# First transformer layer as one stream of 64 pairs of heads, with the scores formed a second time with keys on partitions, and softmax weights kept in fp32

## The chip, the cores and the metric

One core of a Trainium2 chip runs the whole program in one launch. The metric is the device time in microseconds (us), median of several executions of the same program. TensorE multiplies matrices into PSUM (8 banks of 128 partitions x 512 fp32), VectorE (DVE), ScalarE (ACT) and GpSimd (POOL) do the elementwise work, and SyncE (SP) issues the DMA transfers. PEld in the profile is TensorE's load of the stationary operand, PE its product.

## The reference, cut to what matters

Two transformer layers over `x` of shape (4, 512, 512). The change touches the first one only: attention with 32 heads of width 16 that share one key and one value head, a linear position bias, a causal mask, and then a linear layer.

```python
x = x + _layernorm(_L0_attn_ref(_layernorm(x), Wq, Wkv, Wo))
x = x + _layernorm(_L0_ffn_ref(_layernorm(x), q_scales, q_vals, bias))

# _L0_attn_ref
q = (hidden_states @ Wq).reshape(b, s, 32, 16)
kv = hidden_states @ Wkv
k, v = kv[..., :16], kv[..., 16:]
scores = jnp.einsum('bqhd,bkd->bhqk', q, k) * scale
bias = slopes[:, None, None] * (pos[None, None, :] - pos[None, :, None])
scores = jnp.where(causal[None, None], scores + bias[None], -jnp.inf)
attn = jax.nn.softmax(scores, axis=-1)
out = jnp.einsum('bhqk,bkd->bqhd', attn, v).reshape(b, s, h)
return out @ Wo
```

## The kernel before

The program has four parts in time: a stage that splits the weights into fp16 high and low halves (`split_matrices`, line 181) and multiplies two fp32 matrices of the second layer (`FusedUpProjections.multiply`, line 796); `layer0` (line 193); the attention of the second layer; its feed-forward part. Only `layer0` is touched.

Every product of activations and weights runs in fp16 as three passes, high x high, low x high, high x low (`product`, line 398). Every transpose is a TensorE instruction on fp32 data against an identity, evacuated twice: ScalarE writes the high half, VectorE subtracts it and writes the low half.

`layer0` calls `run(b, attend, back, front)` for b = -1, 0, 1 and 2 (a hardware loop), 3, 4. A call with `attend` computes the heads of batch b, and, dealt out over its steps, the output projection and linear layer of batch b-1 (`back`) and the first normalisation of batch b+1 (`front`). Between calls all engines meet in `clear`. One step handles one head:

- `stack_queries` (lines 443 and 444, once per two heads) copies the queries of two heads into 128 rows; ScalarE evacuates them at line 535.
- `scores` (line 459) multiplies by the stacked keys, queries on partitions, 512 + 384 + 256 + 128 columns, the causal triangle of 128-blocks.
- GpSimd makes the table of position biases and mask (line 371); VectorE adds it to the score, writes the sum to SBUF and takes the row extreme in the same instruction (`biased`, line 680).
- ScalarE takes the exponential in SBUF with the extreme as bias (line 575).
- TensorE transposes the ten 128x128 blocks (line 472); ScalarE (line 543) and VectorE (line 708) write the fp16 high and low halves to `pT`.
- `weigh_values` (line 484) forms 30 products per head, each with a 128x128 fp16 block of weights as stationary operand and 17 columns of values (16 and a column of ones for the row sum) as moving operand; ScalarE copies the 68 columns to `ob` (line 550).

Sums are divided out per batch (lines 649 and 652). Layer normalisations are VectorE's work (statistics, line 592; scaling, line 603; addition, line 612), except that GpSimd computes the power -1/2 (line 359) and scales `x_front` (line 363). PSUM banks go round in the order of a list of uses: a use takes the bank that the use eight places before it has left, and `take(u)` waits until that one is evacuated.

Of the kernel before, what the change touches and what calls it, by code (L numbers as in the profile page):

```python
# [29 lines left out]
ALU = mybir.AluOpType  # L30
# [8 lines left out]
P = 128  # L39
# [153 lines left out]
def layer0(nc, A, W0, C, xT, x2_dram):  # L193
# [5 lines left out]

    with ExitStack() as stack:  # L200
        sc = Scope(nc, stack)
        xb = sc.sb("xb", [P, TT, D])
        yb = sc.sb("yb", [P, TT, D])
        xf = sc.sb("x_front", [P, TT, D])
        aT = [sc.sb("front_T_hi", [P, KT, S], F16), sc.sb("front_T_lo", [P, KT, S], F16)]
        bT = [sc.sb("back_T_hi", [P, KT, S], F16), sc.sb("back_T_lo", [P, KT, S], F16)]
        khi = sc.sb("khi", [P, S], F16)
        kst = sc.sb("kst", [P, S], F16)
        kab = sc.sb("kab", [P, 2, S], F16)
        v2 = sc.sb("v2", [P, TT, 2 * EV], F16)  # L210
        qT = [sc.sb("qT_hi", [P, KT, S], F16), sc.sb("qT_lo", [P, KT, S], F16)]
        stk = sc.sb("stk", [P, 2, S], F16)
        tab = sc.sb("tab", [P, 4, S])
        xp = sc.sb("xp", [P, 4, TRIW])
        pT = [sc.sb("pT_hi", [P, 3, NBLK, P], F16), sc.sb("pT_lo", [P, 3, NBLK, P], F16)]
        ob = sc.sb("ob", [P, TT, H0, EV])
        nm = sc.sb("nm", [P, 4, TT])
        rsum = sc.sb("rsum", [P, TT, H0])
        st = sc.sb("st", [P, TT, 6])
# [3 lines left out]
        cs = sc.sb("cs", [P, 1])  # L223
        cinv = sc.sb("cinv", [P, 1])
        cy = sc.sb("cy", [P, 1])
        banks = [sc.ps(f"bank{i}", [P, S]) for i in range(8)]

        s_x = sc.sem("s_x_loaded")
        s_dv = sc.sem("s_dve_steps")
        s_ya = sc.sem("s_y_out")  # L230
        s_yf = sc.sem("s_y_filled")
        s_xf = sc.sem("s_front_loaded")
        s_nf = sc.sem("s_front_normed")
        s_kv = sc.sem("s_keys_values_ready")
        s_ve = sc.sem("s_variance")
        s_rs = sc.sem("s_rstd")
        s_xn = sc.sem("s_normed_rows")
# [3 lines left out]
        s_sf = sc.sem("s_s_filled")  # L241
        s_sh = sc.sem("s_s_hi_out")
        s_kf = sc.sem("s_stack_filled")
        s_sd = sc.sem("s_s_freed_by_dve")
        s_sa = sc.sem("s_stack_ready")
        s_tab = sc.sem("s_table")
        s_ex = sc.sem("s_exp")
        s_pf = sc.sem("s_pv_filled")
        s_pd = sc.sem("s_pv_out")
        s_on = sc.sem("s_heads_normed")  # L250
        s_out = sc.sem("s_x_stored")

        def score_fills(h):

            return [("s", h, i) for i in range(3 - h % 2)]

        def score_fill(h, t):

            return ("s", h - h % 2, 2) if t == 1 else ("s", h, 0 if t == 3 else 1)

        Q_AT = {0: 1, 9: 2, 11: 3}
        Y_AT, N2_AT = (1, 3, 5, 7), (12, 13, 14, 15)
        F_AT, N3_AT = (17, 19, 21, 23), (28, 29, 30, 31)
        N1_AT = (16, 18, 20, 22)

        wq, wkv, wo, wf = W0["wq"], W0["wkv"], W0["wo"], W0["wf"]
        GQ, GKV, GO, GF = range(4)  # L270
        gm = W0["gm"]

        def run(b, attend, back, front):

            extra = {}
            if attend:
                extra.update({h: [("q", m)] for h, m in Q_AT.items()})
                if back:
                    for kind, at in (("y", Y_AT), ("n2", N2_AT), ("f", F_AT), ("n3", N3_AT)):
                        extra.update({h: [(kind, t)] for t, h in enumerate(at)})  # L280
                if front:
                    extra.update({h: [("n1", t)] for t, h in enumerate(N1_AT)})

                front_pieces = {2: (0,)}
                back_pieces = {8: (0,), 9: (1,), 10: (2,), 24: (3,), 25: (4,), 26: (5,)}
                pool_pieces = {2: ["n1"]} if front else {}
                if back:
                    pool_pieces.update({8: ["rstd"], 9: ["rstd"], 24: ["rstd"], 25: ["rstd"]})
                steps = H0 + 2
            else:  # L290
                for h, kind in enumerate(("y", "n2", "f", "n3") * back + ("n1",) * front):
                    extra[2 * h] = [(kind, t) for t in range(TT)]
                front_pieces = {-1: (0,)}
                back_pieces = {1: (0, 1, 2), 5: (3, 4, 5)}
                pool_pieces = {0: ["rstd"] * (front + 4 * back)}
                steps = 8 if back else 2

            uses = [("K",), ("V",), ("q", 0)] * attend + [("o", t) for t in range(TT)] * back
            uses += ([("stack", 0)] + score_fills(0)) * attend
            for h in range(steps):
                if attend:
                    uses += [("T", h - 1, i) for i in range(3)] * (1 <= h <= H0)
                    uses += [("stack", h // 2 + 1)] * (h % 2 == 0 and h // 2 + 1 < PAIRS)
                    uses += [("pv", h - 2)] * (h >= 2)
                    uses += score_fills(h + 1) if h + 1 < H0 else []
                uses += extra.get(h, [])
            slot = {u: n for n, u in enumerate(uses)}  # L310


            signals = {k: (s_tf, s_tl) for k in ("n1", "T", "o", "n2", "n3")}
# [1632 lines left out]
```

## Time and profile before

| | us |
|---|---|
| median of 3 executions | 2516.77 |
| lowest, highest | 2516.7, 2525.8 |
| the profiled execution, its own time | 2520.12 |
| its span, first to last instruction | 2518.3 |
| granted TensorE clock, mean over the span | 0.944 of full speed |

The span is the part of the profiled execution that the trace divides; 1.8 us lie around it. Rows of a stretch give, in order: its bounds, its length, the busy time of PE, PEld, DVE, ACT and POOL with the number of instructions, the granted TensorE clock (1.00 is 2.4 GHz, 0.50 is 1.2 GHz), the share of the DMA engines and GB/s. A group of instructions gives line, engine, operation, tiles, shapes and count, then busy time, mean duration in ns, and the idle time of the engine before them with its releaser.

### The profile page before, as it was taken

The numbers are of one execution on the slowest core, as the hardware profiler recorded it, in microseconds if no ns is written. First come the engines' busy times: TensorE is split into PE (matmuls) and PEld (weight loads), VectorE is DVE, ScalarE is ACT, GpSimd is POOL, SyncE is SP. The second block draws the span as 40 slices with busy tenths as digits, with TensorE's granted clock in tenths as the row PEclk, the third lists the DMA queues.
The fourth block names the chain that finished last, engine by engine and source line by source line (L and its number), as shares of the span: only waits on it lengthen the run. The fifth ranks groups of instructions, "written<-read, shape, count | busy, mean of one in ns | idle before, by whom it ended". The sixth has DMA issues, their size and how long they took to land. (4 is left out here: it accounts for less than half of the span.)

```text
span 2518.3 us, 49756 instructions
## 1 busy us (share of the span) xinstructions
PE 2146.9 (85%) x18352; PEld 1310.3 (52%) x18352; DVE 1864.5 (74%) x4645; ACT 1531.5 (61%) x3606; POOL 688.4 (27%) x563
## 2 busy tenths in 40 slices
PE   6688777778774589999999999999999999758997
PEld 2465555555552255555555555655555556423443
DVE  3688897897995477777777777777777777575554
ACT  2587776777771376667667676667666767341221
POOL 0312212111110243343433343334333333112221
PEclk9899899889997799999999999999999999978999
DMA  5101001000000343444334434443344333320000
GB/s 203 33 2 35 1 7 47 2 18 18 2 18 17 115 81 63 89 87 91 80 66 89 81 71 82 80 91 78 64 89 84 66 68 65 72 87 17 34 17 34
DMA packets 380593, 147.59 MB, mean 59 GB/s; under 512 B 354928, under 2 KB 359664, under 8 KB 378304
## 3 DMA queue, kind: packets, MB, share of 16 engines
q1 hardware_dynamic: 380352, 144.41, 25.5%
q8 instruction: 147, 2.41, 0.4%
q14 instruction: 94, 0.77, 0.1%
HBM read 48.95 MB, written 11.53 MB: 24 GB/s over the span
## 5 line engine op out<-in xcount | busy, mean ns | idle before, releaser
L1157 ACT ACTIVATE xp<-xp,nm 128x128 f32<-128x128 f32 (+3 forms) x512 | 281.3, 550 | 354.5 <-DVE nm L1236 354.5
L1017 POOL TENSOR_TENSOR q_in_sbuf<-q_in_sbuf,sinq 128x512 f32<-128x512 f32 x128 | 231.2, 1806 | 688.2 <-ACT q_in_sbuf L1145 581.3
L1207 DVE SCALAR_TENSOR_TENSOR probs_lo<-xp,rl,probs_hi 128x128 f16<-128x128 f32 (+3 forms) x512 | 263.5, 576 | 109.4 <-ACT probs_hi L1122 109.4
L575 ACT ACTIVATE xp<-xp,nm 128x512 f32<-128x512 f32 (+3 forms) x512 | 249.8, 569 | 50.9 <-DVE nm L680 49.1
L680 DVE CUSTOM_DVE_ANT_0 xp<-bank,tab,cs 128x512 f32<-128x512 f32 (+3 forms) x512 | 250.2, 545 | 4.3 <-PE bank L459 2.0
L1236 DVE CUSTOM_DVE_ANT_0 xp<-bank,mask,cs 128x128 f32<-128x128 f32 (+3 forms) x512 | 250.3, 545 | 0.0
L1122 ACT ACTIVATE probs_hi<-xp,rl 128x128 f16<-128x128 f32 (+3 forms) x512 | 244.0, 549 | 0.7 <-DVE rl L1256 0.7
L472 PE MATMUL bank<-ident,xp 128*128 128x128 f32 x1280 | 182.7, 291 | 62.6 <-ACT xp L575 45.6
L1041 PE MATMUL bank<-xT_hi,wq_hi 128*128 128x512 f16 x512 | 195.2, 381 | 43.2 <-DVE yacc L1251 37.4
L708 DVE TENSOR_TENSOR pT_lo<-bank,pT_hi 128x384 f16<-128x384 f32 (+1 forms) x384 | 207.1, 593 | 32.5 <-ACT pT_hi L543 32.4
L1041 PE MATMUL bank<-p1T_hi,v_hi 128*128 128x128 f16 x1280 | 223.0, 220 | 2.9 <-DMA p1T_lo<-probs_lo 2.9
L1041 PE MATMUL bank<-p1T_hi,v_lo 128*128 128x128 f16 x1280 | 222.9, 220 | 0.0
L1041 PE MATMUL bank<-p1T_lo,v_hi 128*128 128x128 f16 x1280 | 222.8, 220 | 0.0
L543 ACT ACTIVATE pT_hi<-bank 128x384 f16<-128x384 f32 (+1 forms) x384 | 181.0, 537 | 57.0 <-PE bank L472 55.0
L1024 POOL TENSOR_TENSOR qf<-q_in_sbuf,t 128x512 f32<-128x512 f32 x160 | 204.3, 1277 | 31.2 <-POOL q_in_sbuf L1017 19.0
L472 PEld LDWEIGHTS bank<-ident,xp 128*128 128x128 f32 x1280 | 150.4, 148 | 99.9 <-issue 27.9
L371 POOL TENSOR_SCALAR tab<-rel,cinv 128x512 f32<-128x512 f32 x128 | 92.5, 725 | 390.0 <-DVE nm L680 318.3
L1041 PE MATMUL bank<-xT_hi,wq_lo 128*128 128x512 f16 x512 | 195.2, 381 | 0.0
L1041 PE MATMUL bank<-xT_lo,wq_hi 128*128 128x512 f16 x512 | 195.0, 381 | 0.0
L1041 PE MATMUL bank<-wo_hi,o1T_hi 128*128 128x512 f16 x512 | 194.0, 379 | 1.1 <-issue 1.1
L1041 PE MATMUL bank<-wo_lo,o1T_hi 128*128 128x512 f16 x512 | 194.0, 379 | 0.0
L1041 PE MATMUL bank<-wo_hi,o1T_lo 128*128 128x512 f16 x512 | 194.0, 379 | 0.0
(235 smaller groups left out, 5535.9 us busy)
## 6 DMA issues: line engine op xcount, KB each, us to landing
raw_q<-in_wq SPq DMA_DIRECT2D x8, 1024.0 KB, 5.3
raw_o<-in_wo SPq DMA_DIRECT2D x8, 1024.0 KB, 5.6
x_front<-in_x SPq DMA_DIRECT2D x4, 1024.0 KB, 5.8
xb<-in_x SPq DMA_DIRECT2D x4, 1024.0 KB, 7.1
x_scratch<-xb SPq DMA_DIRECT2D x4, 1024.0 KB, 4.4
x_before<-x_scratch SPq DMA_DIRECT2D x4, 1024.0 KB, 5.6
wup<-in_wup SPq DMA_DIRECT2D x3, 1024.0 KB, 11.9
fused_scratch<-fused SPq DMA_DIRECT2D x12, 256.0 KB, 2.4
```

The costliest lines, as they stand in the source:

```text
L472: last = pe.transpose(bank[:, at:at + P], xp[:, h % 4, TRI[t] + j * P:TRI[t] + (j + 1) * P], C["ident"][:, :])
L543: act.activation(pT[0][:, h % 3, COLD[js[0]]:COLD[js[0]] + n, :], bank_of(("T", h, i))[:, 0:n * P].rearrange("p (t c) -> p t c", c=P), ACT ...
L575: act.activation(x, x, ACT.Exp, scale=-1.0, bias=nm[:, h % 4, t:t + 1]).then_inc(s_ex, 1)
L680: ins = dve.tensor_tensor_reduce(out=xp[:, h % 4, TRI[t]:TRI[t] + w], in0=bank_of(u)[:, at:at + w], in1=tab[:, h % 4, S - w:S], scale=cs[: ...
L708: dve.tensor_tensor(pT[1][:, h % 3, c, :], bank_of(u)[:, 0:n * P].rearrange("p (t c) -> p t c", c=P), pT[0][:, h % 3, c, :], ALU.subtract) ...
L1017: pool.tensor_tensor(qs[:, i % 2, :], qs[:, i % 2, :], rope["sink" if u[0] == "k" else "sinq"][:, :], ALU.mult).then_inc(s_rot, 1)
L1024: pool.tensor_tensor(qf[:, i % 2, :], qs[:, i % 2, :], t2[:, i % 2, :], ALU.add).then_inc(s_qf, 1)
L1041: ins = pe.matmul(out, lhs(a), rhs(c), start=(first and i == 0), stop=(last and i == 2))
L1122: ins = act.activation(pr[0][:, m % 2, c], xp[:, m % 3, c], ACT.Copy, scale=rl[:, m % 3, t:t + 1])
L1157: ins = act.activation(x, x, ACT.Exp, scale=-1.0, bias=nm[:, m % 3, t:t + 1], accum_out=ls[:, m % 3, t:t + 1])
L1207: ins = dve.scalar_tensor_tensor(pr[1][:, m % 2, c], xp[:, m % 3, c], rl[:, m % 3, t:t + 1], pr[0][:, m % 2, c], ALU.mult, ALU.subtract)
L1236: ins = dve.tensor_tensor_reduce(out=xp[:, m % 3, TRI[t]:TRI[t] + w], in0=bank_of(("s", m, i))[:, col:col + w], in1=mask[:, S - w:S], scal ...
```

## The change

`layer0` is rewritten; the rest of the program is untouched. Its calls of `run` become one block without a barrier, a loop over steps n = -16 to 91. Pair p of heads (64 in all, 16 per batch) passes through it in three places: scores and maxima at step p, exponents at step p + 6, products with the values at step p + 7. Each step also holds one piece of the other work of some batch.

- Scores are formed with queries on partitions, only for their maximum. The query stack holds, per head, 64 rows: the high and low halves, the slope beside a row of positions, and rows for the maximum. It is put together by 24 DMAs per four pairs instead of by TensorE and ScalarE. The position bias is thus part of the product. The mask is written to the bank by a product of a diagonal with a triangle before it. The two heads of a pair use rows 0 to 63 and 64 to 127 of the array.
- VectorE takes the maxima with five reductions of 512 columns per pair, and writes nothing else. The maxima of four pairs are transposed once, split in halves and put into the query stack by four DMAs.
- The scores are formed again with keys on partitions, minus the maximum through those rows: the exponents, already transposed. ScalarE takes five exponentials of 512 columns per pair straight from PSUM and writes fp32 weights `px`. Tables, transposes and both halves of `pT` are gone.
- `weigh_values` uses the fp32 weights as they are: 20 products per pair, stationary 128x128 fp32, 17 moving columns of fp32.
- Layer normalisations scale on ScalarE, add on GpSimd; the division by the sums is on GpSimd.

The diff, cut to its core:

```diff
-            uses = [("K",), ("V",), ("q", 0)] * attend + [("o", t) for t in range(TT)] * back
-            uses += ([("stack", 0)] + score_fills(0)) * attend
...
+        X_LAG, V_LAG, N_LAG = 6, 7, 8
+        for n in STEPS:
+            if 0 <= n < NP:
+                fillings += [("s", n, i) for i in range(5)]
+            if 0 <= n - V_LAG < NP:
+                fillings.append(("pv", n - V_LAG))
+            if n % GP == 0 and 0 <= n // GP - 1 < NG:
+                fillings.append(("m", n // GP - 1))
+            if 0 <= n - X_LAG < NP:
+                fillings += [("x", n - X_LAG, i) for i in range(5)]
+            fillings += others(n)
...
+                def take(u):
+                    i = place[u]
+                    if i >= 8:
+                        pe.wait_ge(*emptied[fillings[i - 8]])
+                    return banks[i % 8]
...
+                def weigh_values(p):
+                    out = take(("pv", p))
...
+                    pe.wait_ge(*emptied[("x", p, 4)])
+                    for e in range(2):
+                        for t in range(TT):
+                            for j in range(t + 1):
+                                i, c = block_of(e, j, t)
+                                ins = pe.matmul(out[:, (TT * e + t) * EV:(TT * e + t + 1) * EV], px[:, p % 3, i, c:c + P],
+                                                v2[:, p // PAIRS % 2, j, :], start=(j == 0), stop=(j == t))
...
+                for n in STEPS:
+                    if 0 <= n < NP:
+                        mask_scores(n)
+                        scores(n)
+                    if 0 <= n - V_LAG < NP:
+                        weigh_values(n - V_LAG)
+                    if n % GP == 0 and 0 <= n // GP - 1 < NG:
+                        turn_maxima(n // GP - 1)
+                    if 0 <= n - X_LAG < NP:
+                        mask_exponents(n - X_LAG)
+                        exponents(n - X_LAG)
+                    for u in others(n):
+                        fill(u)
...
+                for n in STEPS:
+                    for u in others(n - 1):
+                        evacuate(u)
+                    for u in norms_at(n):
+                        normalise(u)
+                    if 0 <= n - X_LAG < NP:
+                        exponentials(n - X_LAG)
+                    if 0 <= n - V_LAG < NP:
+                        copy_heads(n - V_LAG)
```

The first loop over steps is TensorE's, the second ScalarE's. `mask_scores` and `mask_exponents` take their five banks, one product each of 128 or 256 columns (1024 in all), before the eight products of `scores` or `exponents` (2560 columns in all). `exponentials` waits for the first two banks together and for the other three together.

## Rows read from the trace of the kernel before

**Rows 1.** The page: the span, and the busy share of each engine.

```profile
span 2518.3 us, 49756 instructions
...
PE 2146.9 (85%) x18352; PEld 1310.3 (52%) x18352; DVE 1864.5 (74%) x4645; ACT 1531.5 (61%) x3606; POOL 688.4 (27%) x563
```

**Rows 2.** Busy time, clock, DMA by stretch: stage start, second batch, tail, first layer.

```profile
62.00:80.00 18.00, 6.15 (x22) 4.15 (x23) 7.71 (x17) 2.39 (x4) 3.50 (x5) 0.50 0.26 66
...
219.00:398.00 179.00, 142.44 (x1692) 99.88 (x1692) 159.42 (x455) 127.39 (x299) 37.46 (x41) 0.91 0.06 19
...
759.00:827.00 68.00, 33.06 (x144) 19.70 (x144) 39.25 (x81) 9.92 (x16) 4.04 (x4) 0.71 0.09 32
62.00:827.00 765.00, 575.57 (x6768) 404.72 (x6768) 639.01 (x1824) 510.47 (x1192) 137.76 (x160) 0.89 0.05 18
```

**Rows 3.** Groups by line and shape, VectorE: line, names, shapes, count, busy us, mean ns, idle.

```profile
L708 DVE TENSOR_TENSOR pT_lo<-bank,pT_hi 128x384 f16<-128x384 f32 x256 | 130.3, 549 | 31.7 <-ACT pT_hi L543 31.6
...
L592 DVE BATCH_NORM_STATS2 st<-yb 128x6 f32<-128x512 f32 x32 | 19.7, 680 | 11.1 <-ACT yb L563 11.0
```

**Rows 4.** The same view, TensorE products and weight loads (PEld).

```profile
L472 PE MATMUL bank<-ident,xp 128*128 128x128 f32 x1280 | 182.7, 291 | 62.6 <-ACT xp L575 45.6 <-DVE qT_lo L644 12.7 <-DVE pT_lo L708 2.4
L472 PEld LDWEIGHTS bank<-ident,xp 128*128 128x128 f32 x1280 | 150.4, 148 | 99.9 <-issue 27.9 <-DVE pT_lo L708 19.6 <-DVE nm L680 16.6
...
L484 PE MATMUL bank<-v,pT_hi 128*128 128x17 f16 x2560 | 116.9, 171 | 21.8 <-DVE nm L680 16.6 <-DVE pT_lo L708 4.8
...
L484 PEld LDWEIGHTS bank<-v,pT_hi 128*128 128x128 f16 x2560 | 112.5, 97 | 31.1 <-DVE nm L680 18.1 <-DVE pT_lo L708 6.3 <-issue 0.8
```

**Rows 5.** Line 796, the fp32 product: durations min, median, max; then two weight loads.

```profile
L796 PEld LDWEIGHTS fu_bank<-wup,wdk x96: 186/190/337, 9.1 to 54.4; 128*128 128x128 f32 x96
L796 PE MATMUL fu_bank<-wup,wdk x96: 592/592/1194, 9.1 to 54.8; 128*128 128x512 f32 x96
...
30.02 0.19 PEld L796 LDWEIGHTS fu_bank<-wup,wdk 128*128 128x128 f32 x1 [0.24 <-issue]
30.45 0.19 PEld L796 LDWEIGHTS fu_bank<-wup,wdk 128*128 128x128 f32 x1 [0.24 <-issue]
```

**Rows 6.** Timeline (start, length, engine, line): ten transposes; two fp16 products.

```profile
113.36 1.15 PEld L472 LDWEIGHTS bank<-ident,xp 128*128 128x128 f32 x10 [0.79 <-issue]
113.39 1.35 PE L472 MATMUL bank<-ident,xp 128*128 128x128 f32 x10 [0.48 <-ACT xp L575]
...
80.88 0.38 PE L398 MATMUL bank<-front_T_hi,wkv_hi 128*128 128x512 f16 x1
...
81.10 0.38 PE L398 MATMUL bank<-front_T_hi,wkv_lo 128*128 128x512 f16 x1
```

**Rows 7.** ScalarE: timeline of eight copies and of four exponentials; then two groups.

```profile
40.71 3.99 ACT L803 ACTIVATE fused<-fu_bank 128x512 f32<-128x512 f32 x8
...
300.14 1.90 ACT L575 ACTIVATE xp<-xp,nm 128x512 f32<-128x512 f32 x4
...
L550 ACT ACTIVATE ob<-bank 128x68 f32<-128x68 f32 x128 | 29.6, 231 | 7.6 <-PE bank L484 7.4
...
L563 ACT ACTIVATE yb<-bank,cy 128x512 f32<-128x512 f32 x16 | 11.0, 688 | 23.4 <-PE bank L398 23.4
```

**Rows 8.** Stretches before and after two falls of the granted clock (seventh column).

```profile
114.50:117.90 3.40, 2.33 (x39) 1.43 (x38) 2.58 (x11) 2.87 (x6) 2.19 (x4) 1.00 0.00 0
118.00:121.00 3.00, 3.00 (x41) 2.53 (x40) 3.00 (x10) 2.37 (x7) 0.69 (x2) 0.50 0.02 5
...
282.00:285.30 3.30, 0.00 (x0) 0.00 (x0) 3.27 (x6) 0.20 (x1) 0.00 (x0) 0.99 0.00 0
286.00:289.00 3.00, 1.83 (x33) 1.10 (x33) 2.97 (x14) 1.70 (x3) 2.02 (x3) 0.50 0.00 0
```

**Rows 9.** The first score evacuation of the layer, VectorE's timeline.

```profile
88.82 0.75 DVE L680 CUSTOM_DVE_ANT_0 xp<-bank,tab,cs 128x512 f32<-128x512 f32 x1 [1.97 <-PE bank L459]
```

More of the change, by code:

```diff
@@ new lines, in layer0 @@
+        far = sc.sb("far", [P, P], F16)
+        tri = sc.sb("tri", [P, 2, P], F16)
+        trit = sc.sb("tri_T", [P, 2, P], F16)
+        row = {n: sc.sb(f"row_{n}", [P, 1]) for n in ("hi", "lo", "pos", "max")}
+        sl = sc.sb("slopes", [P, H0])
+        slh = sc.sb("slopes_hi", [P, H0], F16)
+        slq = sc.sb("slopes_32", [P, 2, H0])
+        col = sc.sb("slope_rows", [P, PAIRS])
+        unit = sc.sb("unit", [P, 1])
+        runit = sc.sb("runit", [P, 1])
+        fq = sc.sb("fq", [P, 1])
@@ L251, in layer0 @@
         s_out = sc.sem("s_x_stored")
[L253 to L270, printed above, removed]
@@ new lines, in _, with hi4, evacuate @@
+            @block.scalar
+            def _(act):
+                act.wait_ge(s_st, 1)
+                act.wait_ge(s_io, 1)
+                for i in range(PAIRS):
+                    ins = act.activation(qs[:, i // GP, i % GP, :], pos[:, :], ACT.Identity, scale=0.0,
+                                         bias=col[:, i:i + 1])
+                ins.then_inc(s_st, 1)
+                def hi4(u):
+                    act.wait_ge(*filled[u])
+                    kind, b, t = u
+                    if t == 0 and kind == "n1" and b >= 2:
+                        act.wait_ge(*filled[("q", GP * (b - 2) + 3)])
+                    if t == 0 and kind == "o" and b >= 1:
+                        act.wait_ge(*last_of("f", b - 1))
+                    if t == 0 and kind == "n2":
+                        act.wait_ge(*last_of("y", b))
+                    act.activation(transposed(u, 0), bank_of(u)[:, :].rearrange("p (k c) -> p k c", c=P),
+                                   ACT.Copy).then_inc(s_th, 1)
+                def evacuate(u):
+                    kind, b = u[0], u[1]
+                    if kind in ("n1", "o", "n2", "n3"):
+                        hi4(u)
+                    elif kind == "K":
@@ new lines, in normalise @@
+                def normalise(u):
+                    kind, b = u
+                    src = {"n1": xf, "a1": yb, "a2": yb, "n2": xb, "n3": xb}[kind]
+                    dst = xf if kind == "n1" else yb
+                    act.wait_ge(s_rs, norm_no[u] + 1)
+                    if kind in ("n2", "n3"):
+                        act.wait_ge(s_ad, TT * (add_no["a" + str(int(kind[1]) - 1), b] + 1))
+                    for t in range(TT):
+                        act.activation(dst[:, t, :], src[:, t, :], ACT.Identity, scale=rs[:, t:t + 1],
+                                       bias=nb[:, t:t + 1]).then_inc(s_nm, 1)
@@ new lines, in exponentials, with copy_heads @@
+                def exponentials(p):
+                    if p >= 3:
+                        act.wait_ge(s_pf, p - 2)
+                    for i in range(5):
+                        act.wait_ge(*filled[("x", p, i)])
+                        act.activation(px[:, p % 3, i, :], bank_of(("x", p, i))[:, :], ACT.Exp,
+                                       scale=unit[:, 0:1]).then_inc(s_ed, 1)
+                def copy_heads(p):
+                    g, pp = p // GP, p % GP
+                    act.wait_ge(*filled[("pv", p)])
+                    if g >= 2 and pp == 0:
+                        act.wait_ge(s_on, g - 1)
+                    act.activation(ob[:, g % 2, 2 * pp:2 * pp + 2, :, :].rearrange("p h t e -> p (h t e)"),
+                                   bank_of(("pv", p))[:, 0:2 * TT * EV], ACT.Copy).then_inc(s_pd, 1)
```

942 lines of the change are left out of this document (510 added, 432 removed).

## The prediction

> **What bounds the kernel now.** I read the page first: 2518.3 us, with PE busy 85% and DVE 74% over the whole program [rows 1]. That is an average over stages with different limits, so the second view is the stretches. The first layer is 62 to 827 us, 765 us long: DVE 639 us busy, PE 576, ACT 510 [rows 2]. In the second batch's 179 us DVE is busy 159 (89%), PE 142, ACT 127 at a granted clock of 0.91 [rows 2]: VectorE ends the steps. The groups say with what. Per head it evacuates ten transposed blocks and the scores; the three-block subtraction alone is 256 x 549 ns [rows 3]. Attention, from 80 to 759 us, is 679 us for 64 pairs of heads: 10.6 us a pair, with everything dealt in between. That is the number to beat.
>
> **What comes off VectorE, ScalarE and GpSimd.** DVE loses both evacuations of a pair and gains five reductions of 512 columns. A 512-column read of fp32 took it 680 ns [rows 3], so 5 x 0.68 = 3.4 us at most. ACT: five exponentials. Eight PSUM copies of 512 columns took 3.99 us together at 0.60 for the last, 0.48 us each back to back; four exponentials over 1280 columns with a pointer operand took 1.90; one copy with a pointer scale 688 ns [rows 7]. I take 0.55 us from start to start and 0.69 for the last: 4 x 0.55 + 0.69 = 2.9 us (2.6 by the copies, 3.4 at 5 x 0.69). The copy of 136 columns is 231 ns for 68 [rows 7] plus some, 0.3. Neither engine alone bounds a step: 3.4 and 3.2 us, plus about 1 to 3 us of other pieces, are under 10.6. GpSimd's table goes. Normalisations now on ACT and POOL, and the DMAs of the stacks, have four steps or a whole step of slack; I cost them at nothing. Their cover is the time in which ACT waits for TensorE (below); without it each 512-column scaling costs 0.69 us.
>
> **What comes onto TensorE.** fp16 products of 512 columns start 0.22 us apart at full clock (80.88, 81.10) [rows 6], so 0.43 ns a column. Per pair: masks 2 x 1024 columns, 2 x 0.44 us. Scores and exponents 2560 columns each: 1.10 us one after the other. If the products on the two halves of the array run side by side, the widest of each pair (512 + 384 + 384 + 256) gives 0.66. No row shows such products; I take 1.0 and keep 0.66 to 1.1. By the Trainium skill (TensorE: Matmul & The Clock Gate, Part 3, Packing small matmuls) products on distinct row groups run concurrently; that would be the lower end, and no run here shows it yet.
>
> The weights are the heavy term. Line 796 is the one fp32 product of the trace: 48 products give 96 records, so each fp32 product is two loads and two products, 40 of each a pair. Its load takes 190 ns at full clock, against 97 for fp16 and 148 for the fp32 transposes [rows 4, 5]. If what the fp16 load takes is fixed time, the fp32 load holds the array for the rest, 190 - 97 = 93 ns, and somewhat more. It hides while a product of 512 columns runs (start to start 430 ns) [rows 5]. With 17 moving columns there is nothing to hide it behind. The ten transposes went 1.15 us for ten loads, 0.11 us apart [rows 6]. I take 0.115 us a load, 40 x 0.115 + 0.2 for the first = 4.8 us a pair. Bounds: 0.06, as (148 - 97) would say if this load ran like a transpose's, 2.5 us; and 0.19, every load unhidden, 7.8 us. What it replaces took 60 fp16 products and 20 transposes a pair. The Trainium skill (same page, Weight-path perf modes) says that the fast weight load doesn't work for fp32; by its load of 128 columns at 1.2 per ns the term would be 4.3 us, an estimate. The rows 190 against 97 agree in direction.
>
> **What of it lies on the path.** Two places tie the engines. TensorE's order in step n is: score masks, scores(n), values(n-7), exponent masks, exponents(n-6), other work. Scalar's: exponentials(n-6), then the copy of the values' bank of n-7. Step n+1's third score mask takes the bank eight places back, which is that values' bank. So scores(n+1) can't start until ACT has done all five exponentials of step n and the copy; and values(n+1) wait for the fifth exponential of step n too. ACT in turn has no exponents until TensorE has gone through scores, values and masks. The two alternate. A period, at full clock:
>
> - exponent masks and the first two banks, with two drains and a semaphore: 0.44 + 0.35 + 0.3 = 1.1 us
> - ACT: 2.9 + 0.3 = 3.2 us
> - three score masks, scores, drain: 0.35 + 1.1 = 1.45 us
> - values: 4.8 us
>
> Sum 10.55 us. Other work of TensorE (12 products of 512 columns, 2.6 us) fits beside ACT's 3.2 us. VectorE's 3.4 us of maxima lie beside the 4.8 us of values. So with the clock up a period is just what a pair costs now, 10.6.
>
> Around it: the first score evacuation was at 88.8 us [rows 9]. About 40 tiny chained VectorE operations, the key stack and the first DMAs precede it now; I add 14 us, so 103. Six steps with scores only, 3.2 us each by VectorE, and a first step of exponents: 126. Then 57 full periods, 7 without scores (1.45 less), and the last batch's back part, 68 us before [rows 2], with GpSimd's slower additions 75. At 10.55: 126 + 57 x 10.55 + 7 x 9.1 + 75 = 866 us for an end that was at 827: +39 us.
>
> **The clock.** The granted clock fell to 0.50 after 3.3 us without a product, and also after 3.4 us with PE shown busy 2.33 us [rows 8]. The whole layer had 0.89, with PE busy 576 of 765 us [rows 2]. The new period is thinner. In the values' 4.8 us two passes of 17 columns (15 ns at 0.43 ns a column) stand against each 115 ns; 3.2 us more are ACT's, empty wherever a batch has no other work for the step (most of steps 0 to 24). I expect falls in nearly every period. TensorE's own 7.35 us of a period cost 14.7 at the lower level (a fp32 load 337 ns there against 190, a product 1194 against 592) [rows 5]. I take 40% of this work at the lower level: 7.35 x 1.4 + 3.2 = 13.5 us a period. Then 126 + 57 x 13.5 + 7 x 11.9 + 77 = 1056: +229 us. The share is the weakest number here; 20% gives 12.0 and +145, 70% gives 15.7 and +370. The Trainium skill (same page, Part 1) has the throttled state as the default that activity releases; whether loads alone count as activity, no row here shows.
>
> **The rivals.**
> 1. The clock stays up since loads keep the array occupied: +39 us, 2556. For it: PEld has the array in every ns of the values. Against: at 0.50, from 118 to 121 us, loads were busy 2.53 of 3.0 us [rows 8] and the clock stayed where it was to the end of that stretch. Range -10 to +80.
> 2. Faster: an fp32 load at 0.06 us, values 2.6 us, period 8.35 with the clock up: 126 + 476 + 7 x 6.9 + 73 = 723, -104 us, 2413. It decides from a load under about 0.10 us: the 39 us over 64 periods are 0.61 us each, 0.015 us on each of 40 loads. The overlap of both halves of the array adds to it. Against: 190 ns is the longest load of the trace.
> 3. All of TensorE at the lower level, or loads unhidden at 0.19 with the clock half up: periods of 17 to 18 us, +450 to +510, 2970 to 3030.
> 4. The two engines don't alternate: then TensorE's 7.35 + 2.6 us of other work = 10 us is the bound, within 20 us of before. The list of banks speaks against it.
>
> **How the numbers follow.** Forecast 0.50, all slower. Rival 1 0.24, of it 0.04 within 0.5% (12.6 us, what a measurement of this kernel can tell from no change) and 0.01 faster. Rivals 2 and 4 together 0.14, of it 0.13 faster and 0.01 within. Rival 3 0.12. So faster 0.14, same 0.05, slower 0.81. The profiled execution took 2520.1 us, 3.3 above the median; 2520.1 + 229 is 2749, on the median 2746. The range leaves out rival 2 and the far part of 3: 2535 to 2920.
>
> **What would show it.** In the profile after: the stretch of the first layer 990 us long; a pair every 13 to 14 us; PEld on `px` 40 a pair, 0.11 us from start to start at clock 1.00; ACT idle before the exponentials until TensorE releases it, and the score masks idle until ACT's copy to `ob`; VectorE near 40% busy; a mean granted clock of 0.6 to 0.8 in the stage. A load of 0.06 us, a steady clock, or exponentials running beside the values' products would make it wrong.

## The result and the profile after

| | us |
|---|---|
| before, median of 4 executions | 2520.28 |
| after, median of 4 executions (2753.09 to 2769.36) | 2756.82 |
| after : before, 95% interval | 1.0945, 1.0902 to 1.0989 |
| span of the profiled execution, before and after | 2518.3, 2757.0 |
| granted TensorE clock, mean over the span, before and after | 0.944, 0.862 |

The kernel is 9.5% slower; the forecast was 2746 with a range of 2535 to 2920. One execution of dual_max_first, a run further down, was a slow one of 5365 us, and its median leaves that out. The spans differ by 238.7 us. The first layer's part ends near 1066 us instead of 827, so the whole loss lies in it.

First the page of `after`, the kernel with the change: span, share of each engine (answers [rows 1]), and the three costliest groups of the layer: line, engine, operation, tiles, shapes, count, then busy time, mean ns, idle time of the engine before them with its releaser.

```profile
span 2757.0 us, 44614 instructions
...
PE 2444.1 (89%) x16896; PEld 1515.0 (55%) x16896; DVE 1578.9 (57%) x3534; ACT 1352.8 (49%) x3014; POOL 655.4 (24%) x658
...
L702 ACT ACTIVATE weights<-bank,unit 128x512 f32<-128x512 f32 x320 | 191.9, 690 | 469.7 <-PE bank L554 469.7
L571 PE MATMUL bank<-v,weights 128*128 128x17 f32 x2560 | 390.8, 304 | 5.2 <-ACT weights L702 5.2
...
L571 PEld LDWEIGHTS bank<-v,weights 128*128 128x128 f32 x2560 | 384.9, 242 | 14.4 <-issue 6.0
```

VectorE went from 74 to 57% and ScalarE from 61 to 49%: the relief that the change gives them is there. TensorE went from 85 to 89% of a longer span. The exponentials (L702) stood 469.7 us waiting for TensorE's exponents (L554), and 2560 weight loads of the values (L571), 40 a pair, took 384.9 us.

The stretches of after: start, the stage that has values in it, tail. Columns as in [rows 2].

```profile
143.00:992.00 849.00, 792.26 (x4905) 564.80 (x4904) 279.83 (x544) 280.21 (x517) 79.89 (x183) 0.68 0.06 16
62.00:143.00 81.00, 40.36 (x249) 20.38 (x250) 42.79 (x99) 25.69 (x43) 4.93 (x41) 0.64 0.11 33
992.00:1070.00 78.00, 34.73 (x160) 21.77 (x160) 29.20 (x64) 25.92 (x40) 19.61 (x32) 0.72 0.18 64
```

In the long stretch TensorE is busy 792 of 849 us (93%) at a granted clock of 0.68, VectorE 280 (33%), ScalarE 280. In [rows 2] VectorE had 89% and TensorE 80% at 0.91. A pair takes 849 / 64 = 13.3 us, against 10.6.

Two steps of after side by side, in its timeline. The first has other work of TensorE (L497, the output projection) and its values run at full clock; the second has none.

```profile
396.28 3.00 ACT L702 ACTIVATE weights<-bank,unit 128x512 f32<-128x512 f32 x5 [7.02 <-PE bank L554]
...
401.47 0.83 PE L525 MATMUL bank<-k_stack_max,q_stack 64*128 64x512 f16 x8
...
402.23 4.54 PEld L571 LDWEIGHTS bank<-v,weights 128*128 128x128 f32 x40
402.23 4.64 PE L571 MATMUL bank<-v,weights 128*128 128x17 f32 x40
...
407.77 3.00 ACT L702 ACTIVATE weights<-bank,unit 128x512 f32<-128x512 f32 x5 [5.94 <-PE bank L554]
...
408.53 0.63 PE L497 MATMUL bank<-wo_hi,back_T_lo 128*128 128x512 f16 x1
...
408.96 0.63 PE L497 MATMUL bank<-wo_lo,back_T_hi 128*128 128x512 f16 x1
```

```profile
238.06 3.00 ACT L702 ACTIVATE weights<-bank,unit 128x512 f32<-128x512 f32 x5 [12.56 <-PE bank L554]
...
241.29 0.61 PE L508 MATMUL bank<-tri,far 128*128 128x256 f16 x2 [2.37 <-ACT ob L710]
...
242.05 1.27 PE L525 MATMUL bank<-k_stack_max,q_stack 64*128 64x512 f16 x8
...
243.25 8.61 PEld L571 LDWEIGHTS bank<-v,weights 128*128 128x128 f32 x40 [0.22 <-issue]
...
253.48 1.84 ACT L702 ACTIVATE weights<-bank,unit 128x512 f32<-128x512 f32 x3 [12.24 <-PE bank L554]
```

A load of fp32 weights takes 4.54 / 40 = 0.114 us at full clock and 8.61 / 40 = 0.215 at half. ScalarE starts its exponentials after 5.94 and 12.56 us of idling for TensorE, and in the second step TensorE's third score mask (L508) stands 2.37 us for ScalarE's copy to `ob` (L710): the alternation. From exponentials to exponentials the first step takes 407.77 - 396.28 = 11.5 us and the second 253.48 - 238.06 = 15.4: less work and more time, since the clock is at its lower level in all of the second. Over the stage, TensorE's waits for that copy are these (engine, tile and line, releaser, us in total, times, longest), 47 us together:

```profile
PE bank L508 <- ACT ob L710: 21.3, 9, 2.4
...
PE bank L584 <- ACT ob L710: 14.4, 10, 1.9
...
PE bank L505 <- ACT ob L710: 11.2, 6, 3.4
```

In the first step the products of 512 columns right behind the values start 0.43 us apart, twice the 0.22 of [rows 6]: the clock has fallen at the end of the values. These are stretches of both steps (columns as before):

```profile
402.00:407.00 5.00, 5.00 (x49) 4.85 (x47) 3.76 (x7) 0.00 (x0) 0.00 (x0) 1.00 0.09 21
...
408.00:411.50 3.50, 3.50 (x12) 1.24 (x10) 0.00 (x0) 2.95 (x6) 0.00 (x0) 0.56 0.12 28
```

```profile
244.00:246.00 2.00, 2.00 (x11) 2.00 (x11) 1.80 (x4) 0.00 (x0) 0.00 (x0) 0.50 0.45 125
...
248.00:250.00 2.00, 2.00 (x11) 2.00 (x11) 0.00 (x0) 0.00 (x0) 0.00 (x0) 0.50 0.09 34
250.00:252.00 2.00, 2.00 (x13) 2.00 (x13) 0.00 (x0) 0.00 (x0) 0.00 (x0) 0.50 0.00 0
```

Loads fill the stretches of the second step, 2.00 of 2.00 us, and the clock stays at 0.50 to their end. Loads with 17 columns behind each didn't bring the clock back in these 8 us. That is the question that the prediction had left to its first rival.

### The profile page after: what moved, and what is told of

The parts are those of the page before. It is cut to its first block and busy times, and to the rows that moved or that the text cites. A ratio compares the mean times of both kernels' runs of the same rounds, so it can differ in the third digit from the quotient of the medians.

```text
span 2757.0 us, 44614 instructions
## 1 busy us (share of the span) xinstructions
PE 2444.1 (89%) x16896; PEld 1515.0 (55%) x16896; DVE 1578.9 (57%) x3534; ACT 1352.8 (49%) x3014; POOL 655.4 (24%) x658
## 5 line engine op out<-in xcount | busy, mean ns | idle before, releaser
L702 ACT ACTIVATE weights<-bank,unit 128x512 f32<-128x512 f32 x320 | 191.9, 690 | 469.7 <-PE bank L554 469.7
L571 PE MATMUL bank<-v,weights 128*128 128x17 f32 x2560 | 390.8, 304 | 5.2 <-ACT weights L702 5.2
L571 PEld LDWEIGHTS bank<-v,weights 128*128 128x128 f32 x2560 | 384.9, 242 | 14.4 <-issue 6.0
L1188 PE MATMUL bank<-kT_hi,q1T_hi 128*128 128x128 f16 (+3 forms) x512 | 148.6, 303 | 18.7 <-DVE q1T_lo L1362 18.7
L464 POOL TENSOR_TENSOR heads_normed<-ob,ro 128x64 f32<-128x64 f32 x128 | 33.1, 294 | 539.0 <-DVE ro L875 539.0
L1188 PE MATMUL bank<-kT_lo,q1T_hi 128*128 128x128 f16 (+3 forms) x512 | 155.4, 303 | 0.0
L1188 PE MATMUL bank<-kT_hi,q1T_lo 128*128 128x128 f16 (+3 forms) x512 | 155.3, 303 | 0.0
## 6 DMA issues: line engine op xcount, KB each, us to landing
wup<-in_wup SPq DMA_DIRECT2D x3, 1024.0 KB, 11.9
```

Of the source, the lines that this page charges most:

```text
L464: ins = pool.tensor_tensor(on[:, :, c:c + E0], ob[:, g % 2, h, :, 0:E0], ro[:, g % 2, h, :].unsqueeze(2).to_broadcast([P, TT, E0]), ALU.mult)
L571: ins = pe.matmul(out[:, (TT * e + t) * EV:(TT * e + t + 1) * EV], px[:, p % 3, i, c:c + P], v2[:, p // PAIRS % 2, j, :], start=(j == 0), ...
L702: act.activation(px[:, p % 3, i, :], bank_of(("x", p, i))[:, :], ACT.Exp, scale=unit[:, 0:1]).then_inc(s_ed, 1)
L1188: ins = pe.matmul(out, lhs(a), rhs(c), start=(first and i == 0), stop=(last and i == 2))
```

## The experiments

Ratios are to the kernel before, timed beside it on the same chip (its median there 2520 to 2527). All but fp16_single and fp16_unchained, which leave out the low halves of weights and values, compute the whole of the reference. The stretch from 160 to 600 us holds more pairs in a faster run; over the whole stage with values in it, the clock is 0.68 in after (143 to 992 us) and 0.85 in wide64 (145 to 907).

| run | median us | ratio (95%) | clock, 160 to 600 us |
|---|---|---|---|
| after | 2756.8 | 1.0945 (1.0902 to 1.0989) | 0.67 |
| wide64 | 2673.1 | 1.0603 (1.0559 to 1.0647) | 0.81 |
| copy_first | 2711.9 | 1.0761 (1.0739 to 1.0784) | 0.69 |
| unchained | 2713.9 | 1.0752 (1.0723 to 1.0781) | 0.68 |
| fp16_single | 2452.8 | 0.9722 (0.9702 to 0.9741) | 0.84 |
| wide64_unchained | 2585.9 | 1.0254 (1.0237 to 1.0271) | 0.90 |
| wide32 | 2759.2 | 1.0945 (1.0927 to 1.0963) | 0.65 |
| fp16_unchained | 2428.3 | 0.9626 (0.9606 to 0.9645) | 0.83 |
| split4 | 2819.1 | 1.1172 (1.1152 to 1.1192) | 0.66 |
| dual_exp | 2593.0 | 1.0278 (1.0252 to 1.0304) | 0.72 |
| dual_wide64 | 2595.7 | 1.0284 (1.0258 to 1.0310) | 0.85 |
| dual_wide64_late | 2605.9 | 1.0324 (1.0299 to 1.0348) | 0.84 |
| dual_max_first | 2587.4 | 1.0242 (1.0215 to 1.0268) | 0.85 |

**wide64: the clock by itself.** The values get 47 columns of zeros, so each product moves 64 columns; loads and order stay.

```diff
-        v2 = sc.sb("v2", [P, 2, TT, EV])
+        VW = 64
+        v2 = sc.sb("v2", [P, 2, TT, VW])
...
+                pool.memset(v2[:, :, :, EV:VW], 0.0)
```

> Edit: each values product moves 64 columns instead of 17 (47 of them zeros that nobody reads); nothing else. More work for TensorE, under the same 40 fp32 loads a pair. Theory (the clock falls because a load-bound stretch streams only two passes of 17 columns per 112 ns): the two passes of 64 columns are 53 ns at full clock and stay hidden behind the next load, the granted clock of the layer rises from 0.68 to 0.85 or more, a period falls from 13.2 to 10.7 to 11.8 us, and the time from 2757 to 2640 to 2690 us. Rival A (the clock falls because TensorE waits for ScalarE once per period, or for lack of anything but columns): clock and time as after, 2745 to 2775. Rival B (loads and products of fp32 do not overlap, so each product adds its columns): 40 x 39 ns x 64 pairs = 100 us longer at full clock, 2850 or more.

Measured: 2673.1, 84 us under after, as the theory had it. Two neighbouring steps of wide64, its timeline:

```profile
404.32 3.00 ACT L704 ACTIVATE weights<-bank,unit 128x512 f32<-128x512 f32 x5 [6.30 <-PE bank L556]
...
405.01 0.38 PE L499 MATMUL bank<-wo_lo,back_T_hi 128*128 128x512 f16 x1
...
405.23 0.38 PE L499 MATMUL bank<-wo_hi,back_T_hi 128*128 128x512 f16 x1
...
408.80 4.54 PEld L573 LDWEIGHTS bank<-v,weights 128*128 128x128 f32 x40
408.80 4.68 PE L573 MATMUL bank<-v,weights 128*128 128x64 f32 x40
...
414.37 1.26 ACT L704 ACTIVATE weights<-bank,unit 128x512 f32<-128x512 f32 x2 [6.30 <-PE bank L556]
```

The 40 loads take 4.54 us as before: the added columns are free behind them. The products of 512 columns are again 0.22 us apart (405.01, 405.23), and the period is 414.37 - 404.32 = 10.05 us, where after had 11.5 for such a pair. More columns, less time, and nothing else differs in these rows but the clock. The Trainium skill (TensorE: Matmul & The Clock Gate, Part 1, HAM oscillation) tells of a kernel whose clock falls while TensorE waits for DMA transfers, and advises to keep TensorE busier there, by the order of the loop or by padding M. Here the clock fell with TensorE 93% busy, which that section doesn't describe, and wider products alone raised it.

**wide32: half the padding.** The same edit with `VW = 32`.

> Edit: 32 moving columns in the values' products instead of 17 (15 of them zeros), order as in after. A dose between after (17 columns, 2757 us, clock 0.68 in the main stretch) and wide64 (2673, 0.85). Theory that the share of a load's time in which columns stream decides (14 ns of 112 in after, 27 here, 53 in wide64): if it acts by degrees, 2700 to 2735 and a clock of 0.72 to 0.80; if there is an edge above 27 ns, 2745 to 2770 and 0.68; if below, 2665 to 2685 and 0.85. Rival (it was not the columns but something else in wide64): 2745 to 2770 as well, and no clock change.

Measured: 2759.2, the clock at 0.65: no gain at all. So 15 columns of zeros do nothing here where 47 do, and the strided copy to `ob`, which both have, isn't what helps wide64.

**copy_first and unchained: the alternation.** ScalarE copies the values' bank before its exponentials instead of after them; in unchained the values also come a step later.

```diff
+                    if 0 <= n - V_LAG < NP:
+                        copy_heads(n - V_LAG)
                     if 0 <= n - X_LAG < NP:
                         exponentials(n - X_LAG)
-                    if 0 <= n - V_LAG < NP:
-                        copy_heads(n - V_LAG)
```

```diff
-        X_LAG, V_LAG, N_LAG = 6, 7, 8
+        X_LAG, V_LAG, N_LAG = 6, 8, 8
```

> Edit: in ScalarE's step the copy of the values' bank goes ahead of the five exponentials, so that the third score mask of the next step no longer waits for the exponentials; the wait of the values for the fifth exponential stays. Theory (the layer is bound by TensorE's own work at a half-lowered clock, and the idle time in front of the score masks is about 34 us in the layer by the waits): 20 to 60 us less than 2757, 2697 to 2737, clock of the layer within 0.04 of 0.68. Rival (the alternation of TensorE and ScalarE sets the period): all of masks and scores, 1.5 to 2.7 us a pair, moves beside the exponentials: 90 to 170 us less, below 2667.

> Edit: the copy first, as in copy_first, and the values' products one step later (lag 8 instead of 7), so that no product of TensorE waits for an exponential of the same step. Theory: TensorE then never waits in a period; the layer is the sum of its own work, 867 us busy in 1008 with start and tail in it, so 60 to 110 us less than 2757, 2647 to 2697, unless the closed gaps also lift the clock (then down to 2600). Rival (alternation is the cause of the whole loss): the layer gets as short as before or shorter, 2520 or less.

Measured: copy_first 45 us under after, as its theory had it. unchained, at 43 us, is no better than copy_first and misses the 60 to 110 of its theory. The stage with values in it, of unchained (columns as before):

```profile
156.00:959.00 803.00, 777.74 (x4868) 555.93 (x4867) 276.73 (x540) 284.07 (x515) 83.47 (x194) 0.70 0.07 18
```

TensorE is busy 777.7 of 803 us. There was little to win: after had only 849 - 792 = 57 us in which TensorE stood, 0.9 us a pair. copy_first left 33 of them (stage 803 us, TensorE busy 769.6; the other half of its gain is work that ran at a clock of 0.71 instead of 0.68), unchained 25. In both, TensorE's waits for the copy to `ob` are down from 47 us to under 1. So the alternation is real and small. It is small since in a step with other work TensorE's twelve products of 512 columns take 12 x 0.43 = 5.2 us if all of them run at the lower level, which outlasts ScalarE's 3.2 us.

**wide64_unchained: both together.**

> Edit: 64 moving columns in the values' products (47 of them zeros that nobody reads) together with the reordering of unchained (copy of the values' bank before the exponentials, values one step later). Theory (two separate costs: thin loads pull the clock down, and once the clock is up the wait for ScalarE is no longer hidden by slow TensorE work): the gain of the two is more than the sum of the single gains over after (83 and 43 us). A period becomes TensorE's own work at full clock, about 7.0 us without and 9.7 us with other work in the step; the time falls by 190 to 230 us from 2757, to 2527 to 2567, clock of the layer's main stretch 0.93 or more. Rival (the clock also falls from other causes, and gains only add): 2620 to 2645 with the clock at 0.85 to 0.88.

Measured: 2585.9, 171 us under after, where the two edits alone gave 84 and 43. The 44 us beyond the sum have two parts. In wide64, where TensorE is done sooner, its waits for the copy to `ob` are 68 us (lines 507, 510 and 586) instead of 47; here they are 1.2. And with less standing between the products the clock is 0.90 instead of 0.81 (1.00 between 600 and 680 us). The expectation was missed by 19 us on the slow side; its mechanism held. This is still 2.5% slower than before, with TensorE busy 409 of 440 us, 303 of them beside weight loads.

**fp16_single and fp16_unchained: the loads.** The weights and the values are kept in fp16; their low halves are left out.

```diff
-        v2 = sc.sb("v2", [P, 2, TT, EV])
-        px = sc.sb("weights", [P, 3, 5, S])
+        v2 = sc.sb("v2", [P, 2, TT, EV], F16)
+        px = sc.sb("weights", [P, 3, 5, S], F16)
```

> Edit: the exponentials write fp16 and the values are fp16, so the values' products are 20 fp16 products a pair instead of 40 fp32 records; the low halves of weights and values are left out. Theory (fp32 loads are the heavy term): the values' stretch goes from 4.6 us at full clock and 8.7 at half to about 0.6, a period from 13.2 to 6.5 to 8.5 us, the time from 2757 to 2350 to 2460 us. Rival (the alternation or the clock sets the time, the loads only fill waits): under 150 us less, above 2600.

> Edit: fp16 weights and values with the low halves left out, as in fp16_single, together with the reordering of unchained. In fp16_single a period is 8.3 us, TensorE is busy 403 of 535 us and waits for ScalarE's copy before the score masks. Theory (with the loads gone, the alternation of TensorE and ScalarE is what bounds): a period falls to 6.2 to 7.2 us, set by ScalarE's 3.3 us plus its other work or by VectorE's 3.2 plus its own, 2330 to 2390 us. Rival (the reordering gains as little as it did in after, 43 us or less): 2410 to 2453.

Measured: 2452.8, 304 us under after and 2.8% faster than before. The values of a pair in its trace:

```profile
411.12 0.57 PEld L571 LDWEIGHTS bank<-v,weights 128*128 128x128 f16 x20
```

20 loads in 0.57 us against 40 in 4.54: an fp16 load costs 0.029 us, a quarter, and there are half as many. Over the layer the values' products keep TensorE busy 43 us instead of 391. Its whole busy time in the stage fell by 389 us, from 792 to 403; the 41 beyond the values' 348 I put down to the clock, 0.83 over the stage against 0.68. Of the 389 us, 75 turned into standing (132 us against 57). So the fp32 loads are what makes the change slow. It doesn't follow that the rewritten layer is the faster one at full precision: the old layer keeps the low halves, and these two runs leave them out. fp16_unchained gained 25 us more, not the 60 to 120 of its theory, and lies in the range of its rival. Between 160 and 600 us its TensorE waits 31 us for VectorE's maxima and its ScalarE 38 us for GpSimd's shifts and 80 for exponents; which of these holds the chain isn't shown.

**split4: full precision with fp16 products.** VectorE casts the fp32 weights to a high half; GpSimd subtracts four of the five low halves, VectorE one; 60 fp16 products a pair.

```diff
+                def weights_hi(p):
...
+                        dve.tensor_copy(pw[0][:, p % 2, i, :], px[:, p % 2, i, :]).then_inc(s_wh, 1)
...
+                def weights_lo(p):
...
+                        pool.tensor_tensor(pw[1][:, p % 2, i, :], px[:, p % 2, i, :], pw[0][:, p % 2, i, :],
+                                           ALU.subtract).then_inc(s_wp, 1)
```

> Edit: the exponentials stay fp32, and VectorE copies each tile to fp16 (high half), GpSimd subtracts for four of the five tiles and VectorE for one (low half); the values get their low half back; the values' products are 60 fp16 products a pair, three passes as in the kernel before; order as in unchained. Nothing is left out. Theory: the values take 60 x 25 ns = 1.5 us; VectorE 3.2 + 5 x 0.35 + 0.7 us plus 1.3 of other work, GpSimd 4 x 1.27 + 1.3 us; a period of 7 to 8.5 us, 2380 to 2470 us, below both kernels. Rival (GpSimd and VectorE hinder each other in SBUF, or the new chain over four engines outlasts a step): 9.5 us or more, above 2510.

Measured: 2819.1, the slowest of all, as its rival had it. Its groups between 160 and 600 us, and one step of its timeline:

```profile
L485 POOL TENSOR_TENSOR weights_lo<-weights,weights_hi 128x512 f16<-128x512 f32 x124 | 164.2, 1352 | 219.5 <-DVE weights_hi L871 219.5
...
L871 DVE CAST weights_hi<-weights 128x512 f16<-128x512 f32 x153 | 131.1, 915 | 5.8 <-ACT weights L722 5.0
L874 DVE TENSOR_TENSOR weights_lo<-weights,weights_hi 128x512 f16<-128x512 f32 x31 | 47.2, 1524 | 1.1
```

```profile
403.50 4.63 DVE L871 CAST weights_hi<-weights 128x512 f16<-128x512 f32 x5
...
403.99 5.15 POOL L485 TENSOR_TENSOR weights_lo<-weights,weights_hi 128x512 f16<-128x512 f32 x4 [10.64 <-DVE weights_hi L871]
```

VectorE's cast takes 0.92 us in the mean and its subtraction 1.52 while GpSimd works beside it. Both stand ahead of the maxima in VectorE's order, and TensorE's exponent masks waited 147 of the 440 us for a maximum. For the cast this trace tells by itself whether the operation is slow: the first one, from 403.50, is done in 0.41 us, before GpSimd starts at 403.99, and over the layer the 320 casts took 0.36 us at least and 1.37 in the median. For the subtraction the next run tells.

**dual_exp: GpSimd out of the splitting.** ScalarE takes each exponential twice, to fp32 and to fp16; VectorE subtracts, behind its maxima.

```diff
+                        act.activation(px[:, p % 2, i, :], bank_of(("x", p, i))[:, :], ACT.Exp, scale=unit[:, 0:1])
+                        act.activation(pw[0][:, p % 2, i, :], bank_of(("x", p, i))[:, :], ACT.Exp,
+                                       scale=unit[:, 0:1]).then_inc(s_ed, 1)
```

> Nothing of the computation is left out. ScalarE takes each exponential twice from the same bank, once to fp32 and once straight to the fp16 high half; VectorE subtracts (five low halves a pair, behind the maxima in its order); GpSimd has no part in it. TensorE multiplies 60 fp16 products a pair instead of 20 fp32 ones; values one step later, copy of heads first. The question is whether the 1.52 us that VectorE's subtraction and the 0.92 us that its cast took in the run before (split4) belong to the operation or to the work of GpSimd beside it. Theory (GpSimd beside it): a subtraction takes 0.55 to 0.75 us here; VectorE has 5 x 0.68 of maxima, 5 x 0.65 of low halves and 1.2 of other work, 7.9 us a pair; ScalarE has ten exponentials at 0.6, 0.3 for the copy and 1.1 of other work, 7.4 us, and it waits 1.1 us for the first two banks of exponents, as their banks are its own last ones: 8.5 us a pair, 9.5 with the clock down. End of the layer at 137 + 57 x 9 + 7 x 7 + 77 = 776 instead of 1068: 2465, range 2420 to 2520, so at or below the kernel before. Rival (the operation itself is that slow): 5 x 1.5 + 3.4 + 1.2 = 12.1 us of VectorE a pair, end near 1000: 2650 to 2720.

Measured: 2593.0, between both. The duration is decided all the same, by four rows of VectorE and GpSimd in its timeline:

```profile
403.79 3.08 DVE L860 TENSOR_TENSOR weights_lo<-weights,weights_hi 128x512 f16<-128x512 f32 x5
```

```profile
479.34 6.31 POOL L478 TENSOR_TENSOR xb<-xb,yb 128x512 f32<-128x512 f32 x4 [0.93 <-ACT yb L701]
...
479.59 7.21 DVE L860 TENSOR_TENSOR weights_lo<-weights,weights_hi 128x512 f16<-128x512 f32 x5
...
486.12 0.68 DVE L860 TENSOR_TENSOR weights_lo<-weights,weights_hi 128x512 f16<-128x512 f32 x1
```

Five subtractions take 3.08 us (0.62 each) by themselves. Beside GpSimd's four additions the first four of five take 486.12 - 479.59 = 6.5 us, 1.6 each; the fifth, shown by itself in the last row, starts after the additions have ended (485.65) and takes 0.68 again. GpSimd's additions take 6.31 / 4 = 1.58 us each there. In after, where VectorE is idle or takes statistics beside them, four take 4.94 to 4.96 us (1.24 each), and so do the last three groups of dual_exp, after the last subtraction. The two engines hinder each other, both ways. The Trainium skill (SBUF — State Buffer, Who interferes with whom) says that a VectorE instruction with two inputs in SBUF contends with a GpSimd instruction that reads SBUF; these rows agree.

The time lies 73 us above the theory's range. A pair took 11.0 us (40 pairs between 160 and 600 us). That is more than ScalarE's 7.4 or VectorE's 7.9, so neither is busy all the time. That they follow each other in part, since three engines pass eight banks round, is a reading and not shown.

**dual_wide64, dual_wide64_late, dual_max_first: which order holds it.** The padding of wide64 on dual_exp; then ScalarE's scalings of the normalisations that no addition follows, behind its exponentials; then VectorE's maxima ahead of its statistics.

```diff
                     for u in norms_at(n):
-                        normalise(u)
+                        if u[0] in ("a1", "a2"):
+                            normalise(u)
...
+                    for u in norms_at(n):
+                        if u[0] not in ("a1", "a2"):
+                            normalise(u)
```

> As dual_exp (nothing left out), with the values padded by zeros to 64 columns, so that each of the 60 fp16 products of a pair moves 64 columns instead of 17. In dual_exp the granted clock was 0.72 between 160 and 600 us and a pair took 10.9 us. A product of 64 columns is 27 ns at full clock, about what one took there with 17 (1.5 us for 60), so the padding costs under 0.3 us a pair. Theory (the clock answers to the columns that move, with fp16 products too): mean clock 0.85 or above in that stretch, score and exponent work of TensorE that lies in the chain with VectorE's maxima and ScalarE's exponentials gets 0.6 to 1 us shorter a pair, 2530 to 2565. Rival (the pauses of TensorE set the clock here, not the thin products; VectorE and ScalarE hold the chain): clock under 0.78 and 2580 to 2605.

> As dual_wide64, and ScalarE's four scalings of a normalisation (the first, third and fifth kind, not those before an addition) come behind the exponentials of their step instead of ahead of them. In dual_exp ScalarE stood 40 us of the 440 between 160 and 600 us waiting for GpSimd's power and shift (29.1 us for the back part, 11.2 for the front), at the head of its queue, with ready banks of exponents behind it. Theory (this wait is on the chain): these 40 us go, some 60 over the layer, of which two thirds are gained: 30 to 60 us under dual_wide64, thus 2475 to 2530. Rival (VectorE's late statistics are what is late, and the maxima behind them): the wait turns up at another place and it is within 12 us of dual_wide64.

> As dual_wide64_late (2606; nothing left out), and VectorE takes the five maxima of a step ahead of the statistics of a normalisation and of the low halves, where the statistics and the variance (2.5 + 0.6 us) stood ahead of them. In dual_exp TensorE's exponent masks stood 3.4 us at 401.5 and 1.9 us at 494.0 for a maximum that VectorE reached only after the statistics, and ScalarE waited up to 7.7 us for the shift that follows them. Theory (the order on VectorE holds the chain maxima, exponents, exponentials): 12 normalisations of 16 steps' batches have their 3 to 8 us taken out of the chain, some 40 to 70 us in all: 2535 to 2570. Rival (any engine's wait is covered by the next one, since three engines share eight banks): within 15 us of 2606.

Measured: 2595.7, 2605.9, 2587.4. In dual_wide64 the clock rose from 0.72 to 0.85 as its theory said, and the time stayed as its rival said: neither had both. TensorE was busy 319 instead of 331 of 440 us, so the clock's gain turned into standing. A higher clock gained nothing here, where TensorE stands for more than a quarter of the time. Later scalings cost 10 us instead of giving 30 to 60, within the 12 of their rival. The earlier maxima gave 18 us, a little more than the 15 of their rival and less than half of the 40 to 70 of their theory. None of these two orders alone is the bound; what is, stays open.

## Why the prediction was right

**The bound and the per-pair sum.** The forecast for the 64 pairs was 57 x 13.5 + 7 x 11.9 = 853 us, the measured stage is 849, and the first layer's loss was forecast as 229 us and is 239. The mechanism is the forecast one: fp32 loads that nothing hides, and a clock that they pull down. That the sum is so near is in part luck, as shown below. The terms, one by one:

- Values, 4.8 us at full clock from 0.115 a load: 4.54 from 0.1135. The choice between 0.06 and 0.19, by the transposes of [rows 6], was the one that mattered, and it held.
- At the lower level a load took 0.215 us. A pair's loads averaged 384.9 / 64 = 6.01 us, so (6.01 - 4.54) / (8.61 - 4.54) = 36% of the pairs' values ran there, where the forecast had 40%. For all of TensorE's work the share was higher: a mean clock of 0.68 is (1 - 0.68) / 0.5 = 64% of the time at the lower level, which is 0.64 x 0.5 / 0.68 = 47% of the work, by an estimate that leaves out the standing.
- Scores, 1.0 to 1.1 us for 2560 columns: the values follow 402.23 - 401.47 = 0.76 us after the first of the eight products, where one after the other these would need 1.10. The halves of the array do run side by side, near the lower end of the bounds (0.66).
- ScalarE: five exponentials 3.00 us (2.9), the copy 0.31 (0.3). VectorE: five reductions of 0.68 (0.68), 33% busy (40%).
- Full clock: the sum said 10.55 us a pair; wide64, at 1.00, shows 10.05, in the links of the sum: ScalarE 3.2 us (3.2), the score mask that waits for `ob` to the values 1.25 (1.45), values 4.5 (4.8), exponent masks to exponentials 1.05 (1.1). The half microsecond is that of the values and the scores.
- The side case of a 20% share was mis-added: 126 + 57 x 12.0 + 7 x 10.3 + 76 is 958, which is +131 and not +145. The forecast doesn't use it.

**The alternation was mis-weighted, and another term made up for it.** This is the step of the sum that failed. It put ScalarE's 3.2 us wholly between TensorE's pieces, and let 2.6 us of other work hide beside them at no cost. At half clock that work takes twice as long (products 0.43 us apart) and outlasts ScalarE; only 57 us in all, 0.9 a pair, were left in which TensorE stood. The rest of the 3.2 us was filled by TensorE itself. 7.35 x 1.4 + 3.2 = 13.5 should have been 12.4 busy + 0.9 standing. The sum has 2.3 us too much of standing and 2.1 too little of TensorE's work, since it took the other work for free and the share at the lower level too low. That these two nearly cancel is luck. The alternation as the tie held in kind (2.37 us of the score mask on `ob`, 47 us of such waits in the stage). copy_first puts its price at 45 us of the 239, and unchained finds none beyond it.

**The clock.** It fell in nearly every period with other work, and without such work it stayed down (0.50 from 226 to 256 us); the mean of the stage is 0.68, within 0.6 to 0.8. wide64 gives 84 us of its cost back with one cause changed. The prediction thought of thin products and of ScalarE's pause as joint causes. The runs bear that out: between 160 and 600 us taking out the pause alone moved the clock from 0.67 to 0.68, the padding alone to 0.81, both to 0.90.

**The start** was at 109.4 for the first maxima instead of 103, and the first exponentials at 137.3 instead of 126; the tail 74 long (992 to 1066) for 77. The late start of 11 us accounts for the 10 between 229 and 239.

**The rivals.** The first (the clock stays up) falls by the rows from 244 to 252 us: loads in every ns, clock 0.50. The second needed a load under 0.10 us, and it took 0.114. Its 2413 was too fast a price even so: fp16_single, with 0.57 us of loads a pair instead of the rival's 2.6, took 2452.8. The third (all of it at the lower level) needed twice the share of work at the low clock. The fourth, TensorE as the only bound, is nearly what the stage is at the low clock, 93% busy, but its time was that of a clock which stays up.

## What to carry to other kernels

Price a product with few moving columns by its weight load, and take the load's price from a place in the trace where nothing hides it. Where a stage of such products makes the clock fall, pad them as far as the load hides it before anything is reordered: that costs nothing here, and gained only while TensorE was the bound. Compare what TensorE has to do in a step with what the engine beside it needs, at the clock that the step will have, before the wait between them is put into a sum. Before work is dealt to GpSimd to relieve VectorE, see whether both would read SBUF at the same time.

## What the runs showed of the hardware

- An fp32 weight load of 128x128 with 17 columns behind it: 0.114 us from start to start at full clock, 0.215 at half (after); an fp16 load 0.029 at full clock (fp16_single). With two loads a product, such an fp32 product costs eight times an fp16 one.
- 40 products of 64 columns took as long as 40 of 17 (4.68 and 4.64 us), and raised the granted clock between 160 and 600 us from 0.67 to 0.81 (wide64); with 32 columns it was 0.65 (wide32).
- 8 us of uninterrupted weight loads, with 17 columns behind each, left the clock at 0.50 (after, 244 to 252 us).
- VectorE's subtraction of two SBUF tiles of 128x512: 0.62 us alone, 1.6 beside GpSimd's additions, which slowed from 1.24 to 1.58 (dual_exp). VectorE's cast of such a tile from fp32 to fp16: 0.36 us at the least, 1.37 in the median of a run in which GpSimd subtracts beside most of them (split4).
